# The gathered tile's scores and indices move from VectorE to ScalarE and GpSimd, in a graph-neighbour kernel

## The reference

```python
mask = A != 0
scores = jnp.where(mask, -jnp.arange(N), -inf)
vals, idx = jax.lax.top_k(scores, 25)
valid = vals > -inf
feats = jnp.where(valid[..., None], X[idx], -inf)
agg = feats.max(axis=2)
agg = jnp.where((mask.sum(-1) <= 25)[..., None], jnp.maximum(agg, 0.0), agg)
out = relu(concatenate([X, agg], -1) @ W + b)
result = layernorm(X + out)
```

## Time and profile before

| | |
|---|---|
| median of 3 runs | 594.37 us |
| profiled execution | 593.69 us |
| its span | 592.0 us |
| VectorE busy | 529.4 us, 89% |
| TensorE busy | 501.7 us, 85% |
| ScalarE busy | 396.1 us, 67% |
| GpSimd busy | 288.7 us, 49% |
| mean granted TensorE clock | 0.973 |

### The profile page before, as it was taken

The page is one execution under the profiler, slowest core; times in us unless marked ns, Lnnn a source line. Parts: engine busy times, 40 slices in busy tenths (PEclk is TensorE's granted clock), DMA queues, the critical chain, the costliest instruction groups (busy, mean ns, idle before and its releaser), DMA issues.

```text
span 592.0 us, 13844 instructions
## 1 busy us (share of the span) xinstructions
PE 501.7 (85%) x4544; PEld 340.4 (58%) x4544; DVE 529.4 (89%) x973; ACT 396.1 (67%) x751; POOL 288.7 (49%) x462
## 2 busy tenths in 40 slices
PE   1347899989988999889988999889987999889982
PEld 0115576556654677556755667556754667556761
DVE  5647999999998989999999999999998999998894
ACT  3362567657985688657886589657885589546654
POOL 2552365257633575247733566337742376336700
PEclk9998999899998999899999999899998999899997
DMA  8893244456536644366556555475445462021102
GB/s 257 212 219 105 79 133 118 99 128 160 132 75 171 135 129 101 106 156 165 113 115 173 124 113 136 96 162 171 110 117 141 135 135 65 2 60 38 50 9 73
DMA packets 91810, 71.31 MB, mean 120 GB/s; under 512 B 63651, under 2 KB 80294, under 8 KB 91686
## 3 DMA queue, kind: packets, MB, share of 16 engines
q1 hardware_dynamic: 85286, 56.77, 39.6%
q0 software_dynamic: 6400, 13.12, 8.1%
HBM read 50.99 MB, written 4.19 MB: 93 GB/s over the span
## 4 chain that ended last, share of the span: by engine, by line
PE 37%; DVE 36%; issue 12%; DVEq 7%; DMA 4%; ACT 2%; SPq 1%; POOL 0%; POOLq 0%
PE pair L1038 29%; DVE part L781 16%; DVE hot L776 5%; DVE g_feat L854 4%; DMA adj_sb<-in_adj 4%; DVEq L851 3%; DVE g_val L822 2%; DVE agg_t L881 2%; PE misc L1083 2%; DVEq L920 1%; PE p_V L1022 1%; DVE g_score L824 1%; PE misc L1084 1%; DVE hot_high L776 1%; DVEq L988 1%
## 5 line engine op out<-in xcount | busy, mean ns | idle before, releaser
L1038 PE MATMUL pair<-hot,x_part 128*128 128x128 bf16 (+3 forms) x3120 | 411.0, 280 | 37.3 <-DVE part L781 27.9
L1038 PEld LDWEIGHTS pair<-hot,x_part 128*128 128x128 bf16 x3120 | 239.1, 99 | 145.1 <-issue 51.6
L781 DVE TENSOR_REDUCE part<-pair 128x128 f32<-128x1024 f32 (+1 forms) x256 | 279.4, 1100 | 30.0 <-PE pair L1038 28.5
L479 POOL DMA_INDIRECT g_feat<-in_x,g_idx x200 | 193.6, 968 | 131.9 <-issue 86.5
L526 POOL TENSOR_TENSOR y_sb<-relu_sb,x_sb 128x128 f32<-128x128 f32 x64 | 30.0, 469 | 146.2 <-ACT relu_sb L652 145.7
L598 ACT ACTIVATE V<-p_V 128x512 bf16<-128x512 f32 x98 | 57.7, 589 | 64.9 <-PE p_V L1022 64.7
L626 ACT ACTIVATE hot<-V,first_bias 128x1024 bf16<-128x1024 bf16 x56 | 63.9, 1141 | 25.3 <-PE pair L1038 25.3
L776 DVE TENSOR_SCALAR hot<-V 128x1024 bf16<-128x1024 bf16 x224 | 80.3, 380 | 0.0
L591 ACT ACTIVATE mask<-adj_sb 128x1024 bf16<-128x1024 uint32 x56 | 58.7, 1048 | 21.9 <-DMA adj_sb<-in_adj 21.9
L641 ACT ACTIVATE hot<-distance,one 128x1024 bf16<-128x1024 bf16 x56 | 63.9, 1141 | 0.2
L634 ACT ACTIVATE distance<-V,second_bias 128x1024 bf16<-128x1024 bf16 x56 | 63.6, 1135 | 0.0
(11 more groups left out here) (88 smaller groups left out, 408.8 us busy)
## 6 DMA issues: line engine op xcount, KB each, us to landing
adj_sb<-in_adj SPq DMA_DIRECT2D x56, 512.0 KB
g_adj<-in_adj SPq DMA_DIRECT2D x8, 512.0 KB, 4.4
x_sb<-in_x SPq DMA_DIRECT2D x8, 512.0 KB, 4.6
out<-y_sb SPq DMA_DIRECT2D x7, 512.0 KB, 5.2
g_feat<-in_x,g_idx POOLq DMA_INDIRECT x200
maskT<-mask SPq DMA_TRANSPOSE x56
out<-y_sb SPq DMA_DIRECT2D x1, 448.0 KB, 3.0
w_sb<-in_W SPq DMA_DIRECT2D x1, 128.0 KB, 6.2
```

Source lines behind the costliest of these rows:

```text
L479: pool.indirect_dma_start(out=g_feat[w][:, k, :], out_offset=None, in_=x_rows, in_offset=bass.IndirectOffsetOnAxis(ap=g_idx[w][:, k:k + 1] ...
L781: dve.tensor_reduce(part[:, par(q, s), :, p], slots_of(q, s, p).rearrange("f k i -> f i k"), AX.X, ALU.max).then_inc(s_used, 1)
L1038: last = pe.matmul(dst, x_part[:, q, part_no, kb], one_hot, start=(first and part_no == 0), stop=(final and part_no == PARTS - 1))
```

## The change

The scores of batches 1 to 7 are made in step 1 of the batch before by two instructions: ScalarE's Sign of the adjacency tile into the score buffer (`find0`), and GpSimd's product of that with the falling numbers (`score0`). The indices and bounds of these batches are made by five small instructions on GpSimd at the end of step 7 (`index0`). VectorE keeps the rounds of maxima, and all of the first batch's extraction. Semaphores go with that: VectorE waits for the scores ahead of group 1 of step 2, GpSimd for the seventh extraction step, SyncE's next load for the Sign that read the last tile.

```diff
 # SyncE, step 1
-sp.wait_ge(s_ex, LAST_STEP * (2 * i + q) + 1)
+if is_first(i, q):
+    sp.wait_ge(s_score, 1)
+else:
+    sp.wait_ge(s_found, 2 * i + q)
 load_adj0(ni, nq)
 # ScalarE
+def find0(batch):
+    act.wait_ge(s_adj0, 16 * (batch + 1))
+    act.wait_ge(s_ex, SEARCH * batch)
+    nc.scalar.activation(g_score[0][:, :], g_adj[0][:, :].bitcast(U32), ACT.Sign).then_inc(s_found, 1)
 # ScalarE, in step(): behind the relus, ahead of first_rank and second_distance
+if s == 1 and not last:
+    find0(2 * i + q + 1)
 # GpSimd
+def score0(batch):
+    wait(s_found, batch)
+    pool.tensor_tensor(g_score[0][:, :], g_score[0][:, :], falling[:, :], ALU.mult).then_inc(s_score, 1)
+def index0(batch, bp):
+    val, pick, step = g_val[0], g_pick[0], 3 * (batch - 1)
+    wait(s_ex, SEARCH * (batch + 1))
+    pool.tensor_scalar(first0[:, :], val[:, 0:1], 0.0, val[:, 0:1], ALU.is_equal, ALU.add).then_inc(s_index, 1)
+    pool.wait_ge(s_index, step + 1)
+    pool.tensor_scalar(pick[:, :], val[:, 0:K], 0.0, first0[:, :], ALU.is_equal, ALU.mult).then_inc(s_index, 1)
+    pool.tensor_scalar(g_bound[0][:, bp, 0:1], val[:, K:K + 1], 0.0, -BIG, ALU.is_gt, ALU.mult
+                       ).then_inc(s_bound, 1)
+    pool.tensor_scalar(g_bound[0][:, bp, 1:2], val[:, 0:1], 0.0, None, ALU.is_gt).then_inc(s_bound, 1)
+    pool.wait_ge(s_index, step + 2)
+    pool.tensor_tensor(pick[:, :], pick[:, :], val[:, 0:K], ALU.add).then_inc(s_index, 1)
+    pool.wait_ge(s_index, step + 3)
+    pool.tensor_scalar(g_idx[0][:, :], pick[:, :], -1.0, row_base[:, batch:batch + 1], ALU.mult, ALU.add
+                       ).then_inc(s_idx0, 1)
 # GpSimd, in step(): behind the residuals of step 1; behind everything of step 7
+if s == 1 and not last:
+    score0(2 * i + q + 1)
...
+if s == MT and not last:
+    index0(2 * i + q + 1, nq)
 # VectorE
-if st > 0:
-    dve.wait_ge(s_ex, LAST_STEP * batch + st)
+if st == 1:
+    dve.wait_ge(s_score, batch + 1)
+elif st > 1:
+    dve.wait_ge(s_ex, SEARCH * batch + st - 1)
...
-EXTRACT = {1: {4: 0}, 2: {1: 1, 4: 2}, 3: {3: 3}, 4: {3: 4}, 5: {1: 5, 3: 6}, 6: {}, 7: {1: 7, 3: 8}}
+EXTRACT = {1: {}, 2: {1: 1, 4: 2}, 3: {3: 3}, 4: {3: 4}, 5: {1: 5, 3: 6}, 6: {}, 7: {1: 7}}
...
+if (s, p) == (7, 0) and not begin:
+    dve.wait_ge(s_bound, 2 * (2 * i + q))
```

More of the change, by code:

```diff
@@ L35 @@
 LAST_STEP = 2 * ROUNDS
+SEARCH = LAST_STEP - 1
 BANK = 4
@@ L194, in build @@
         g_bound = [sb(f"g_bound{w}", [P, 2, 2], F32) for w in range(2)]
+        first0 = sb("first0", [P, 1], F32)
         g_idx = [sb(f"g_idx{w}", [P, K], I32) for w in range(2)]
@@ L266, in build @@
         s_ex = sem("extraction0_step")
+        s_score = sem("scores0_ready")
+        s_index = sem("index0_step")
+        s_bound = sem("bounds0_ready")
+        s_found = sem("neighbours0_marked")
         s_adj0 = sem("adj0_loaded")
@@ L844, in extraction @@
                     if w == 0:
-                        ins.then_inc(s_ex, 1)
+                        ins.then_inc(s_ex if st > 0 else s_score, 1)
             def gathered_max(w, bp, signal, steps):
@@ L959, in step @@
                         if p in steps:
-                            if steps[p] == 0:
-                                dve.wait_ge(s_ex, LAST_STEP * (2 * i + q + 1))
-                                dve.wait_ge(s_adj0, 16 * (2 * i + q + 2))
                             extraction(0, 2 * i + q + 1, (steps[p],), nq, False)
```

## The result

The changed kernel takes 620.65 us (median of 6, 619.85 to 623.06); the kernel before takes 594.32 us beside it. The ratio is 1.0454 (95% interval 1.0426 to 1.0482): slower by 26 us. The forecast was 619 us, from 603 to 630.

A forecast was written before the change was run, and what follows sets the result against it. The prediction took TensorE to bound steps 2 to 5, with step 1 losses not given back. Stalls 19.7, product 2, clock 4 and indices -0.9 made 24.8 us on 593.7: 618.5, forecast as 619 us, range 603 to 630.

The forecast's parts named there:

- TensorE loses in step 1 for good: Steps 2 to 5 are TensorE's; what it loses in step 1 isn't given back before the batch ends.
- The signs named in advance: Seven sign waits of 3.6 to 5.5 us, V copy waits some 5 us, product 2.0 to 2.6 us.
- The wait at the head of ScalarE's queue: Step 1: the sign waits for the adjacency load and delays the V copy for TensorE; 19.7 us over seven batches.
- the clock, +4: After the new stalls TensorE runs at 1.2 GHz; 1 us for four of seven batches.
- The working for batch 5: Step 1 of batch 5: violations product at 396.0 instead of 390.99, counts at 400.5 instead of 395.99, +4.5 us.
- one short landing: One adjacency load in batches 1, 3 and 5 may land quickest, so 4.0 us was taken for each.
- The product, +2: GpSimd's 1024-column product, ahead of reduction 1 of step 2: 2.3 us long, costing 0.3 us per batch, 2 in all.
- The way in which the product costs: VectorE waits under 1 us for the product before reduction 1 of step 2; one-hots beside it also take longer.
- The indices, -0.9 in batch 7 and hidden elsewhere: Index work leaving VectorE behind step 7 gains 0.9 us in batch 7; elsewhere it hides or a stall covers it.
- The sum: 19.7 + 2 + 4 - 0.9 = 24.8 us added to the profiled execution's 593.7 us, giving 618.5.

The follow-up runs named there:

- the wait alone: Kernel before, plus a ScalarE wait for the gathered tile's load at the head of step 1, nothing moved: 610.75 us, ratio 1.0292.
- TensorE kept busy: Changed kernel, plus 20 matmuls of 512 columns on TensorE ahead of the V copy wait in batches 1, 3 and 5: 618.95 us, ratio 1.0412.
- kernel with the sign late: Changed kernel with ScalarE's sign moved from the head to the end of step 1, behind the second V copy: 592.72 us, ratio 0.9979.
- index half alone: Changed kernel with scores back on VectorE, no sign or product; indices and bounds stay on GpSimd: 590.38 us, ratio 0.9951.
- score half: Changed kernel with indices and bounds back on VectorE; sign on ScalarE and product on GpSimd stay: 619.93 us, ratio 1.0417.

## Why the prediction was right

The steps in their order, each with what the runs say:

- *TensorE loses in step 1 for good.* Right. The 26.9 us that the violations products have lost by batch 6 are the loss of the whole span, 26.1 us, with the 1.0 us that batch 7 gives back. The signs named in advance came too: seven waits of the sign of 3.6 to 5.2 us, waits for the V copy of 5.0, 5.9 and 6.05 us in batches 1, 3 and 5, and a product of 2.36 us.
- *The wait at the head of ScalarE's queue, 19.7 us with the sign, and the clock, +4.* Right in mechanism: one moved instruction takes the loss away, and the wait alone makes 17 us. Together the two terms were 23.7 us, and 25.5 us came in step 1. What was short is batches 1, 3 and 5: 4.0 and 1 for the clock against 5.3, 6.2 and 6.3. The working for batch 5 had 5.0 us at the violations product (396.0 for 390.99) and 4.5 at the counts; the 4.0 allowed for one short landing, and of the three (3.8, 5.0 and 4.6 us) only the first was short. Batches 4 and 6 had 3.1 and 1.4 us in the working at the violations product, and 1.4 and 2.5 came; that the two sums agree (4.5 and 3.9) is in part luck.
- *The clock alone.* The slow level came behind the three long waits (3.95, 3.95 and 3.88 us from the turning to the violations product against 2.5 at the full level, 4.4 us in all), where I had four at 1 us. Against the kernel before the same stretches grew by only 0.1, 1.05 and 1.0 us, since VectorE's violation tests were what TensorE waited for there. That the total follows the clock isn't shown: the run with TensorE kept busy gave the gain back in batches 4 and 6.
- *The product, +2.* The duration was 2.36 us for 2.3. The kernel with the sign late is 2.3 us above the index half alone, which is this term's size, though the intervals of the two just overlap. In the changed kernel itself it can't be seen: all that was lost outside step 1 is 1.3 us in batches 1 to 7, less than the 1.7 us by which one slow stretch in batch 4 moves it. VectorE has more cover there, since it waits twice as long for TensorE's groups as before (the first line is of the changed kernel, the second of the one before):

```profile
DVE part L823 <- PE pair L1081: 60.6, 57, 5.4
```
```profile
DVE part L781 <- PE pair L1038: 28.5, 32, 5.9
```

- *The way in which the product costs* was the other one: not a wait, but one-hots that last until the product is over. The Trainium skill (SBUF — State Buffer, section "SBUF: two separate sides") has it that VectorE in a two-port mode and GpSimd take a shared port pair in turns, and the later of the two waits for the whole of the other's instruction. The trace agrees for the one-hots: 1.25 us instead of 0.42, ended 0.3 us behind the product. Its f32 merge beside the same product was not held up (0.94 us).
- *The indices, -0.9 in batch 7 and hidden elsewhere.* Batch 7 gave back 1.0. They are six operations on GpSimd, not five, but of 0.21 to 0.43 us each, 1.9 us in all where 2.3 were allowed. Alone the half saved 3 us. That is near what TensorE's waits for the violation tests leave room for: it waited 1.69, 0.76, 0.74 and 1.78 us in batches 1, 3, 5 and 7, and 0.97 us less VectorE work in each gives at most 3.4 us (an estimate). In the changed kernel the stalls cover all but batch 7.
- *The sum.* 24.8 us against 26.3. No step failed, but the sum is closer than its terms: the stall in batches 1, 3 and 5 came out larger by 2.8 us with the clock counted, and of the product's 2 us at most 1.3 is there.

## What to carry to other kernels

Before work is moved to an engine that has room, look at the instant and not at the share: what its queue holds behind the new instruction, who waits for that, and whether the input has landed when the queue gets there. A load issued in the same step as its first use may be free on the engine that uses it late in the step and dear on one that uses it at the head. Moving the use to the end of the step gave back all of the 26 us here, and moving the load ahead most of them.

## What the runs showed of the hardware

- Four traces (the changed kernel, the score half, the wait alone, TensorE kept busy) have 26 waits of TensorE for the V copy. Behind all 12 of 3.8 to 6.2 us it turned the features at the slow level (1.46 us for the twelve matmuls), behind all 14 of 0.6 to 3.5 us at the full level (0.84 us); two of the 14 stood behind the added matmuls. In batch 0 of the changed kernel, behind the wait of 3.5 us, the slow level came right after the turning: six matmuls took 2.31 us there instead of 1.46.
- A 1024-column f32 product of two tiles on GpSimd takes 2.36 us, against 1.23 us for VectorE's compare and multiply of the same size; six operations on 25 columns or fewer take 0.21 to 0.43 us each.
- Beside that product VectorE's bf16 one-hots of 1024 columns took 1.25 us instead of 0.42 in five of seven batches, its f32 merge 0.94 us as ever.
- The same kernel took 594 us in most sessions and 693 to 699 us in two, with VectorE and ScalarE as busy as ever and TensorE paused between its instructions.
